# A new opening, and the last block's outer products held back until the second norm

## The reference

```python
x = L0_attn_x
xn = _layernorm(x, axis=-1)
s = _L0_attn_ref(xn, ...)        # causal softmax attention, 16 heads of 64
g = _silu(_L0_ffn_ref(xn, ...))  # 8 experts, one per token, and a shared one, F = 352
x = x + s * g
xn = _layernorm(x, axis=-1)
s = _L1_attn_ref(xn, ...)        # linear attention, 16 heads of 8
g = _silu(_L1_ffn_ref(xn, ...))  # two layers of local attention (8 heads of 64,
x = x + s * g                    # window 64, rotary) with a gated feed-forward
```

```python
kv_cum = jnp.cumsum(k[..., :, None] * v[..., None, :], axis=2)
k_cum = jnp.cumsum(k, axis=2)
out = einsum(q, kv_cum) / (einsum(q, k_cum) + EPS)
```

## Time and profile before

| | us |
|---|---|
| median of 3 executions | 2015.17 |
| lowest and highest | 2014.45, 2017.05 |
| the profiled execution | 2009.89 |
| its span, first to last instruction | 2008.1 |
| busy: TensorE | 1741.9 (87%) |
| busy: VectorE, ScalarE, GpSimd | 1256.6, 1191.0, 851.9 |

### The profile page before, as it was taken

One profiled execution on the slowest core, in us unless ns is written; L12 is line 12 of the kernel. 1 busy time (PEld: TensorE's weight loads), 2 busy tenths in 40 slices (PEclk: granted clock), 3 DMA queues, 4 the chain that ended last, 5 costly groups with the idle time before them and its releaser, 6 DMA issues.

```text
span 2008.1 us, 38006 instructions
## 1 busy us (share of the span) xinstructions
PE 1741.9 (87%) x12538; PEld 1123.2 (56%) x12538; DVE 1256.6 (63%) x4105; ACT 1191.0 (59%) x3559; POOL 851.9 (42%) x985
## 2 busy tenths in 40 slices
PE   6699989998989888998999898988899798785776
PEld 5378754654566546664566456654566455463454
DVE  5244547566675567666766667666766665857764
ACT  3554547566756675657666575666665665453643
POOL 3622226533535343532554353533353255534640
PEclk9999999999989999999999999999999897897978
DMA  8256500000000000000000000000000000000000
GB/s 245 71 180 211 176 16 4 9 1 1 7 1 17 1 7 1 17 1 1 7 1 17 1 7 1 17 1 6 1 7 6 1 7 1 1 7 1 1 1 11
DMA packets 50012, 53.78 MB, mean 27 GB/s; under 512 B 6546, under 2 KB 42396, under 8 KB 49820
## 3 DMA queue, kind: packets, MB, share of 16 engines
q0 software_dynamic: 7808, 27.79, 4.3%
q1 hardware_dynamic: 42012, 23.56, 4.1%
HBM read 41.90 MB, written 9.44 MB: 26 GB/s over the span
## 4 chain that ended last, share of the span: by engine, by line
PE 46%; DVE 20%; ACT 8%; issue 7%; POOL 1%; DVEq 0%; ACTq 0%; POOLq 0%
PE ps L610 5%; PE ps L672 5%; PE ps L756 3%; DVE p L1081 3%; PE ps L589 3%; PE ps L569 3%; DVE big L1264 3%; PE ps L630 3%; PE ps L579 3%; DVE ss L1260 2%; PE ps L807 2%; PE ps L798 2%; PE ps L644 2%; PE ps L654 2%; PE ps L800 2%
## 5 line engine op out<-in xcount | busy, mean ns | idle before, releaser
L1378 POOL COPY rdx<-rden 128x256 f32<-128x256 f32 x256 | 99.6, 418 | 624.4 <-DVE rden L1098 620.0
L1081 DVE CUSTOM_DVE_ANT_0 p<-ps,mask 128x128 f32<-128x128 f32 (+1 forms) x512 | 152.2, 353 | 197.9 <-PE ps L602 176.0
L1081 DVE CUSTOM_DVE_ANT_0 p<-ps,mask,rr 128x128 f32<-128x128 f32 x512 | 148.8, 347 | 168.9 <-PE ps L598 168.8
L610 PE MATMUL ps<-ident,p 128*128 128x128 f32 x1280 | 219.4, 293 | 37.4 <-ACT p L899 30.0
L899 ACT ACTIVATE p<-p,nmax 128x128 f32<-128x128 f32 (+1 forms) x512 | 226.3, 442 | 0.0
L756 PE MATMUL ps<-wqkv,hT 128*128 128x512 f32 x384 | 196.4, 618 | 31.1 <-ACT big L978 25.9
L913 ACT ACTIVATE pt<-ps 128x384 f32<-128x384 f32 (+1 forms) x256 | 111.6, 436 | 180.7 <-PE ps L610 171.5
L898 ACT ACTIVATE p<-p,nmax 128x128 f32<-128x128 f32 x512 | 200.2, 391 | 22.1 <-DVE nmax L1081 21.4
L610 PEld LDWEIGHTS ps<-ident,p 128*128 128x128 f32 x1280 | 140.7, 145 | 116.8 <-issue 101.6
L579 PE MATMUL ps<-ident,big 128*128 128x128 f32 x512 | 86.2, 308 | 80.1 <-DVE big L1269 35.5
L1092 DVE COPY pt<-ps 128x384 f32<-128x384 f32 (+1 forms) x256 | 124.5, 486 | 49.0 <-PE ps L610 45.9
(11 more groups left out here) (260 smaller groups left out, 4060.7 us busy)
## 6 DMA issues: line engine op xcount, KB each, us to landing
slots_in<-xn SPq DMA_DIRECT2D x1, 2560.0 KB, 12.9
v<-slots_in SPq DMA_DIRECT2D x20, 128.0 KB
slots_out<-v SPq DMA_DIRECT2D x20, 128.0 KB
big<-in_x SPq DMA_DIRECT2D x4, 512.0 KB, 5.8
x<-in_x SPq DMA_DIRECT2D x8, 256.0 KB, 3.7
out_x<-x SPq DMA_DIRECT2D x8, 256.0 KB, 2.3
wqkv<-in_wqkv SPq DMA_DIRECT2D x2, 768.0 KB
xn<-in_x SPq DMA_DIRECT2D x6, 256.0 KB, 3.2
```

The lines of the kernel that those rows point to most:

```text
L610: last = nc.tensor.transpose(bank[:, j * P:(j + 1) * P], c.p[:, u % 4, j * P:(j + 1) * P], c.ident[:, :])
L1081: last = V.tensor_tensor_reduce(out=c.p[:, u % 4, a:b], in0=bank[:, a:b], in1=mask, scale=scale, scalar=3e38, op0=ALU.add, op1=ALU.min, ac ...
```

## The change

Opening:

- `e_at` goes from 8 to 10, so the experts start two ticks later. Block 0's eight pairs of layer 0 keep ticks 0 to 15. Block 1's first step comes at tick 30 instead of 22: no attention stands in ticks 16 to 29. In turn the seven empty ticks 32 to 38 behind `down0` go, and block 1's 16 steps run from 30 to 45 without a gap. The first local attention (block 0) starts at tick 49 instead of 47, and everything behind it is two ticks later, otherwise in the same order. At that place `wo`, `down0` and `comb` of block 0 and 1 stand one tick ahead of the first `cum`, not in its tick, and one tick there is without a step.
- For the first five pairs VectorE makes the expansion itself, right behind the inverse; GpSimd does it from pair 5 on.
- `wg 0` comes at tick 9, in GpSimd's order now behind `tables`; before it stood two ticks ahead of them.
- TensorE forms the totals of the sort (`totals`) behind two value tiles, not three.

Last block (7), in ticks of the new list:

- `kv 0` waits for `hn_ready` of block 7's layer 0: the second norm.
- `kv 2` and `kv 3` move from the tick of the third `cum` part to `l0 + 8`, the tick behind `kn`; before, they stood three ticks ahead of it. No wait is added there.
- The four `cum` and `sum` parts of the second sequence come four ticks later, at `l0` + 11 to 14; `o1` two ticks later, at `l0 + 17`, the tick of block 6's `fin`; `oT` and `s1` one tick each behind it. `wo` of the last projection follows in the next tick.

```diff
+EXPERTS_AT = 10
+EARLY_PAIRS = EXPERTS_AT // 2
...
-        e_at = 8
+        e_at = EXPERTS_AT
         start = e_at + SLOT_PAIRS + 6
-        self.fill(start - 2, range(16, 22))
-        self.ticks += [None] * 7
-        self.fill(8, ())
+        self.fill(start - 2, range(16, 30))
+        self.fill(15, ())
...
-            for n, at in enumerate((1, 2, 5, 6, 9, 10, 11, 12)):
+            parts = (1, 2, 5, 6, 11, 12, 13, 14) if b == LAST else (1, 2, 5, 6, 9, 10, 11, 12)
+            for n, at in enumerate(parts):
...
-                        self.put(l0 + at, "kv", b, t)
-            self.put(l0 + 15, "o1", b)
-            self.put(l0 + 17, "oT", b)
-            self.put(l0 + 18, "s1", b)
+                        self.put(l0 + (8 if b == LAST else at), "kv", b, t)
+            o1 = l0 + (17 if b == LAST else 15)
+            self.put(o1, "o1", b)
+            self.put(o1 + (1 if b == LAST else 2), "oT", b)
+            self.put(o1 + (2 if b == LAST else 3), "s1", b)
...
     for t in range(TILES):
-        if t == 3:
+        if t == 2:
             totals()
...
+    def expand(pair):
+        dve.wait_ge(c.rden_ready, pair + 1)
+        if pair:
+            dve.wait_ge(c.mm_full, mm.full("m", pair - 1))
+        spread(V, c).then_inc(c.rdx_ready, 1)
...
                 inverse(plan.step(tick - 1))
+                if plan.step(tick - 1).pair < EARLY_PAIRS:
+                    expand(plan.step(tick - 1).pair)
...
+def spread(eng, c):
+    rd = c.rden[:, :].rearrange("p (s h i) -> p s i h", s=2, h=2)
+    for sq in range(2):
+        out = c.rdx[:, sq * SEQ:(sq + 1) * SEQ].rearrange("p (i h d) -> p i h d", i=2, h=2)
+        last = eng.tensor_copy(out, rd[:, sq, :, :].unsqueeze(3).to_broadcast([P, 2, 2, HD]))
+    return last
...
         elif t == 0 and b == LAST:
             pool.wait_ge(c.mm_full, mm.full("cum", b - 1, 1, LPARTS - 1, 0))
             pool.wait_ge(c.prod_ready, 4 * LPARTS * b)
+            pool.wait_ge(c.hn_ready, plan.turn[(b, 0)] + 1)
...
-        if (st := plan.step(tick - 1)) and st.s == 1:
+        if (st := plan.step(tick - 1)) and st.s == 1 and st.pair >= EARLY_PAIRS:
             expand(st.pair)
```

More of the change, by code:

```diff
@@ L1374, in expand @@
             pool.wait_ge(c.mm_full, mm.full("m", pair - 1))
[L1375 to L1379, removed]
+        spread(G, c).then_inc(c.rdx_ready, 1)
     def scatter(j):
```

## The result

The changed kernel took **2026.76 us** (median of 8, 2025.14 to 2038.23) against 2014.81 for the kernel before (8, 2011.03 to 2020.10): a ratio of **1.007**, 95% interval 1.0057 to 1.0082. That is 11 to 17 us slower, where 7.4 us faster was forecast; it lies outside the range of 1998 to 2016. The profiled execution took 2031.20 us, its span is 2029.4, against 2009.89 and 2008.1 before: +21.3 in this pair of profiles.

A forecast was written before the change was run, and what follows sets the result against it. TensorE, busy 87% of the span, bounds most stages, so only its waits can give time back. Opening -7.8 and last block +0.4 make -7.4 us: 2015.17 to 2007.8 us, with 8 in 10 within 1998 to 2016.

The forecast's parts named there:

- (a): Opening: five expansions leave GpSimd, scatters end at 87.3 us, TensorE's 10.91 us wait for tokens goes; net -10.6 us.
- rival 2: Opening gives little: waits with remote releaser move to the new places, "xT" waits fully; 2012.6, at worst 2017.3; chance 0.22.
- (b): Opening, GpSimd's new order: first weight load behind "tables" lands near 105 us, just when TensorE wants it; 0, at most 4.
- (d): Opening, ticks with experts alone: nine more waits of 1.03 us for VectorE, a tick taking 5.43 us; +9.3 us.
- Rival 3: Expert ticks: the weights can't keep up, 6.8 us a tick at 210 GB/s, +14 us, 2021.5; chance 0.13.
- (e): Opening, block 1 over block 0's first norm: 3.5 of 7.25 us wait left, 1.2 of half clock gone; -5.0 us.
- (g): Last block: kv 0 and 1 wait for the second norm, so three slowed VectorE steps run fast; -6.4 us.
- (h): Last block: kv 2 and 3 leave the second "rr", -7.9, and the third cum part takes back 2.0; -5.9 us.
- (i): Last block: nothing makes kv 2 wait for the normed keys, so VectorE's four products let in three GpSimd instructions; +6.9 us.
- Rival 1: Last block: VectorE keeps the shared port through its four key products, the +6.9 us falls to 0; 2000.9; chance 0.2.
- (j): Last block, sequence two's cums four ticks later: +2.1 beside "ln2n", -1.8 for leaving ticks 299 and 300, +1.0 half clock.
- (k): Tail: "o1" behind block 6's last products, TensorE stands 4 us, returns at half clock; last projection +4.5 us, warm +2.6.

The follow-up runs named there:

- quiet chip: Kernel before and changed kernel, both unchanged, run on one chip whose traces show no late TensorE signals: changed kernel at 1.0014 (0.9994 to 1.0034), +2.8 us.
- noisy pair: The result's own two profiles, kernel before and changed kernel, whose traces show late TensorE signals in the opening: ratio 1.007, profiled 2009.89 and 2031.20 us.

## Why the prediction was wrong, step by step

**(a), the step that failed.** It put the end of the scatters at 87.3 us and the gain at 10.6. The scatters ended at 95.04, and TensorE reached the experts 11.1 us later than before instead of earlier. The rate of issue was right, as the quiet chip shows. Wrong was the sentence that TensorE "now meets ScalarE's own stall", priced at 3.0. That stall was not ScalarE's own. It was a signal of TensorE that came late while GpSimd issued scatters, and the expansions that the change takes away had been pauses in the row. I had seen the mark "remote" and gave it a bound of 6 us (rival 2); it was worth more. From 42 us up to the first expert ticks (118 us, 110 before) TensorE was idle for 20.8 us instead of 22.4, and the clock took 7.6 us instead of 4.2: +1.9 where -10.6 was forecast, half of the 24.8 us between the forecast of the opening and the profile. On the quiet chip the same two sums (to 95 us, 102 before) fell by 10.8 and 2.7 us, so there step (a) gave even more than forecast. By the runs the place of the expansions is worth 7.5 to 12 us.

**(b)** held in its price: the first weights were issued at 113.46, behind a wait of 17.23 us that by GpSimd's order is for `tables`, and TensorE waited 1.38 us for them (0, at most 4). **(c)** cost no VectorE time of note (0.49 us a pair), but see (a).

**(d)** held: eight more waits of up to 1.03 us, +7.2 against +9.3, and a tick of 5.50 us (5.43 was forecast). **Rival 3** is false: at this pace the DMAs kept up.

```profile
195.53 1.58 PE L740 MATMUL ps<-big,v 128*128 128x128 f32 x12 [1.03 <-DVE v L1213]
```

```profile
190.00:222.00 32.00, 27.01 (x228) 25.62 (x228) 12.42 (x23) 10.12 (x23) 11.28 (x12) 1.00 0.83 262
```

**(e)** held in its wait: 3.64 us are left of the 7.25 (3.5 was forecast). Its clock term of 1.2 us did not come: TensorE still came back at half clock. **(f)** held: the wait of 1.56 before the first `cum` is gone.

**A term that was missing.** I followed what the change moves, and not what it leaves without cover. The root of block 0 now stands in a tick with no long work on TensorE: 4.67 us instead of 1.48 before L681. And I priced the clock only where a wait went. From 42 us to the point where the orders agree, the clock took 18.0 us instead of 7.7 in the noisy pair, and TensorE was idle for 51.5 us instead of 45.5. Of these 10.3 us of clock, 3.4 belong to (a); the other 6.9 stand behind the first expert ticks, and there are 8.0 of them in the quiet pair. The forecast had -1.2 there. This is the second mis-sized term, as large as a third of the miss in the noisy pair and most of it in the quiet one. Why it came is only in part known: half clock behind L681 is 1.5 us of it (2.7 on the quiet chip), but more, 4.9 us instead of 1.7 in the noisy pair, stands behind a wait of 2.6 us before a merge that both kernels have (L654 at 394.07, L657 at 407.21).

**(g)** -6.4, measured -6.4 (18.24 late at 1836.71, 11.88 at 1857.79). **(h)** -5.9, measured -6.3: between the matmuls before and the start of the keys, TensorE's lag of 13.0 shrank to VectorE's of 6.8. **(i)** +6.9, measured +6.4, and its opposite, -6.45 of TensorE's wait, once kv 2 waits for the keys. **Rival 1** is false. The Trainium skill's sentence on the shared port (SBUF — State Buffer, "Who interferes with whom") speaks of one whole instruction, and the trace agrees with it so read: between VectorE's four products three of GpSimd get their turn, 9.13 us instead of 2.67. **(j)** +1.3, measured +1.3 up to the transposes behind "ln2n"; its half clock lasted longer, and TensorE lost another 2.0. **(k)** +4.5, measured +4.2 (16.51 at 1977.99, 20.73 at 1997.40). Between (g) and (h) 1.1 us went, about what TensorE's half clock behind the first keys lasted longer (5.8 us lost from 1850 to 1870, 4.6 from 1834 to 1858 before). Sum of the last block: +0.4 forecast, +3.0 measured in the profile, +3.6 by the runs.

Four sums of the prediction don't come out of its own rows. The three long and four short steps of (h) add up to -8.4 and not -7.9, so (h) is -6.4. The three instructions of (i) are 7.05 and not 6.9. The warm case of (k) is +2.1 and not +2.6. And if "xT" waits its full 7.25, (e) gives 5.0 less and not 3.5, so the worst case of rival 2 is 2018.8. None of them changes the direction of the forecast.

**So:** the last block was right in mechanism, and in size to 3 us; that it missed by no more is in part luck, since (h), (i) and (k) came out 1.2 us too dear together and so hid some of the 3.1 us that the clock took behind the first keys and behind "ln2n". The opening was wrong by a wait whose cause I did not ask for, and by the clock behind the experts. Where there are no late signals, the changed kernel comes to +2.8 us (-1.2 to +6.8) instead of -7.4. Rival 2 pointed the right way, but its worst case, 2017.3, was too mild.

## What to carry to other kernels

A wait whose releaser the profile doesn't know is not an engine's own cost: ask what runs beside each one and stops when it ends, before you take away the work that happened to interrupt it. Price the clock on both sides: each of the new or longer standstills here (4.67, 4.01 and 4.19 us) brought TensorE back at 1.2 GHz, which cost another 1.5 to 4.9 us, and give that price a range, since one and the same wait of 2.6 us cost 1.7 us before and 4.9 in the changed kernel. And where work is held back "until" something, check that a wait says so: one line behind `kn_ready` was worth 6.45 us.

## What the runs showed of the hardware

While GpSimd issues indirect scatters (one each 1.26 us), TensorE's signals reach VectorE and ScalarE up to 18.7 us late on some chips. All twelve traces from noisy chips show it and none of the eight from quiet ones, where the kernel before and the changed one both ran. The kernel before takes 2005 us (median) on both quiet chips and 2013 to 2024 on the noisy ones. At the matmul where the orders agree, its noisy trace is 8.3 us behind its quiet one, and that of the changed kernel 24.0.

Pauses in the row shorten the late signals. Five traces with the changed opening have 40.3 to 45.1 us of them, three with the old one, whose rows are of 8 scatters, 23.2 to 36.4, and the one with three pauses of 2.4 us 22.9. A quarter of the bytes doesn't shorten them (45.1). Why chips differ, and what holds the signals, stays open. The trace models the ends of matmuls, so I can't tell a late signal from a product that was late in ending. For the second speaks that TensorE has standstills of its own there: its waits marked "issue" from 50 to 102 us sum to 0.4 to 6.7 us in the noisy traces and to nothing in the quiet ones. Whether the gathers of weights do the same wasn't tried; in six noisy traces a wait of 3.8 to 5.4 us for a signal of TensorE stands beside their first rows, at 120.62 us in the changed kernel.

VectorE and GpSimd take turns, instruction by instruction: four products of VectorE (128x512) take 9.13 us beside three two-input instructions of GpSimd, and 2.67 us when those wait.
